# Small loads of four stages issued one stage earlier in a fused float32 network of attention, routing and spectral layers

## The reference, cut to what matters

```
x = x + neighbourhood_attention(gn(x)) ; x = x + conv_attention(gn(x))
t = tokens(x)
t = t + linear_attention(ln(t))     # q * sum over tokens of (k * v), with biases
t = t + spectral_ffn(ln(t))         # causal convolution with 16 filters by a transform over blocks,
                                    # mixing by 16 + 16 matrices, inverse transform, and a 3-tap part
t = t + causal_attention(ln(t))     # softmax(q k' / sqrt(128)) v over 4096 tokens
t = t + mixture_of_experts(ln(t))   # 8 experts, the best 2 of each token
```

## Time and profile before

| | |
|---|---|
| median of three runs | 3133.16 us |
| time of the profiled execution | 3134.44 us |
| its span, first to last instruction | 3132.4 us |
| TensorE busy | 2877.5 us (92%) |
| VectorE, ScalarE, GpSimd busy | 1936.2, 1436.2, 1073.7 us (62%, 46%, 34%) |
| mean granted clock of TensorE | 0.961 |
| data moved | 213.44 MB, 68 GB/s in the mean |

### The profile page before, as it was taken

One profiled execution on the slowest core, in us unless ns is written; L12 is line 12 of the kernel. 1 busy time (PEld: TensorE's weight loads), 2 busy tenths in 40 slices (PEclk: granted clock), 3 DMA queues, 4 the chain that ended last, 5 costly groups with the idle time before them and its releaser, 6 DMA issues. The chain is left out here.

```text
span 3132.4 us, 61484 instructions
## 1 busy us (share of the span) xinstructions
PE 2877.5 (92%) x23047; PEld 2223.5 (71%) x23047; DVE 1936.2 (62%) x3839; ACT 1436.2 (46%) x3076; POOL 1073.7 (34%) x1108
## 2 busy tenths in 40 slices
PE   5989999589987889999999999999779998999799
PEld 4667777334442558888988988888558887888455
DVE  5555558558846446666666666666457776776465
ACT  2545555321135325555555555555436665667200
POOL 3444445049923035555555555554100000000100
PEclk9999999789989799999999999999879999999899
DMA  7988784000003333444343443433200000000000
GB/s 165 176 175 169 171 172 129 1 14 1 1 3 118 141 66 80 86 85 88 79 88 81 89 88 80 89 81 65 65 7 1 1 1 1 1 1 1 10 22 31
DMA packets 419407, 213.44 MB, mean 68 GB/s; under 512 B 326260, under 2 KB 398604, under 8 KB 417324
## 3 DMA queue, kind: packets, MB, share of 16 engines
q1 hardware_dynamic: 401248, 199.32, 29.1%
q10 hardware_dynamic: 17868, 10.19, 1.7%
HBM read 177.82 MB, written 52.89 MB: 74 GB/s over the span
## 5 line engine op out<-in xcount | busy, mean ns | idle before, releaser
L1795 DVE TENSOR_TENSOR sl_vl_slot<-sl_psV_slot,sl_vh_slot 128x512 fp32r<-128x512 f32 x1024 | 636.1, 684 | 381.1 <-ACT sl_vh_slot L1777 380.8
L1777 ACT ACTIVATE sl_vh_slot<-sl_psV_slot 128x512 fp32r<-128x512 f32 x1024 | 529.5, 605 | 512.4 <-PE sl_psV_slot L1732 511.0
L1750 PE MATMUL sl_psY_slot<-sl_vl_slot,sp_Mh_sp 64*128 64x512 f32 x2048 | 417.2, 389 | 0.8 <-DVE sl_vl_slot L1795 0.3
L1750 PE MATMUL sl_psY_slot<-sl_vh_slot,sp_Ml_sp 64*128 64x512 f32 x2048 | 414.5, 386 | 0.0
L1750 PE MATMUL sl_psY_slot<-sl_vh_slot,sp_Mh_sp 64*128 64x512 f32 x2048 | 414.4, 386 | 0.0
L1708 POOL TENSOR_TENSOR sl_fl_slot<-sl_f_slot,sl_fh_slot 128x512 fp32r<-128x512 f32 x256 | 336.8, 1315 | 20.5
L1706 POOL CAST sl_fh_slot<-sl_f_slot 128x512 fp32r<-128x512 f32 x256 | 166.4, 650 | 451.2 <-PE sl_psV_slot L1732 450.0
L2191 DVE TENSOR_TENSOR ca_ptl_ca<-ca_psT_ca,ca_pth_ca 128x512 fp32r<-128x512 f32 (+1 forms) x272 | 183.8, 676 | 168.4 <-ACT ca_pth_ca L2128 168.3
L2128 ACT ACTIVATE ca_pth_ca<-ca_psT_ca 128x512 fp32r<-128x512 f32 (+1 forms) x272 | 158.8, 584 | 183.2 <-PE ca_psO_ca L87 179.2
L1750 PEld LDWEIGHTS sl_psY_slot<-sl_vl_slot,sp_Mh_sp 64*128 64x128 f32 x2048 | 207.8, 184 | 38.0 <-issue 12.7
L2255 POOL TENSOR_TENSOR ex_pick_ex<-ident 128x8 fp32r<-128x8 f32 x1 | 0.2, 203 | 665.0 <-POOLq L70 665.0
(11 more groups left out here) (397 smaller groups left out, 6260.6 us busy)
## 6 DMA issues: line engine op xcount, KB each, us to landing
sl_f_slot<-filt_hat SPq DMA_DIRECT2D x1024, 64.0 KB, 2.2
na_v_na<-na_windows SPq DMA_DIRECT2D x128, 390.0 KB
na_windows<-na_values SPq DMA_DIRECT2D x160, 113.8 KB, 7.9
na_values<-na_vo_na ACTq DMA_DIRECT2D x32, 260.0 KB, 9.0
u_hat<-fw_o_fwd SPq DMA_DIRECT2D x8, 1024.0 KB, 3.8
sl_u_slot<-u_hat SPq DMA_DIRECT2D x128, 64.0 KB, 2.2
y_hat<-sl_y_slot SPq DMA_DIRECT2D x128, 64.0 KB, 1.8
X<-in_x SPq DMA_DIRECT2D x8, 512.0 KB, 7.8
```

Of the source, the lines that this page charges most:

```text
L1750: mm = e.matmul(psY[half][:, :], left[pl][rows, :], right[pr][rows], start=kc == 0 and k == 0 and x == 0 and z == 0, stop=kc == KC - 1 and ...
L1777: e.activation(v_out(0, n, q), bank(4 * n + q), ACT.Copy).then_inc(S["v_high"], 1)
L1795: e.tensor_tensor(v_out(1, n, q), bank(m), v_out(0, n, q), ALU.subtract).then_inc(S["v_split"], 1)
```

## The change

Four groups of small loads move to the stage ahead of the one that uses them. `linear_attention` and `causal_attention` get their tiles from new helper classes; their normalisations run these helpers on SP. `c_fwd` is loaded at the end of `MixingWeights.sync`. `c_inv` is loaded in `spectral_slots` behind the first filter loads, and its product with `keep` becomes VectorE's last work there. Without being named in the title, EARLY goes from 8 to 4 in both spectral stages: `load_early` brings 4 slots (8 partitions, 256 KB) at a time, 15 times, and leaves 4 slots to the inverse transform.

```
+class LinearInputs:
+    engines = ("sync",)
+    names = ["la_loaded"]
+    def __init__(self, nc, T, ctx):
+        self.T, (sb, _) = T, allocator(nc, ctx, "_la")
+        self.w, self.bias = sb("la_w", [128, 3, 128]), sb("la_b", [128, 3])
+    def sync(self, e):
+        e.dma_start(self.w[:, :, :], self.T["la_w"]).then_inc(self.S["la_loaded"], 16)
+        e.dma_start(self.bias[:, :], self.T["la_b"]).then_inc(self.S["la_loaded"], 16)
+        e.wait_ge(self.S["la_loaded"], 32)
...
 def linear_attention
-            @block.sync
-            def _(e):
-                e.dma_start(w[:, :, :], T["la_w"]).then_inc(S["la_loaded"], 16)
-                e.dma_start(bias[:, :], T["la_b"]).then_inc(S["la_loaded"], 16)
-                e.wait_ge(S["la_loaded"], 32)      # on tensor, scalar and vector
...
 MixingWeights.sync, at its end
+        e.dma_start(self.G["fwd"][:, :, :], T["c_fwd"]).then_inc(S["fwd_loaded"], 16)
+        e.wait_ge(S["fwd_loaded"], 16)
...
 spectral_inputs
-                e.dma_start(fwd[:, :, :], T["c_fwd"]).then_inc(S["fwd_loaded"], 16)
-                e.wait_ge(S["fwd_loaded"], 16)     # on tensor
...
 spectral_slots
-    NPV, NFI, NFR, EARLY = 6, 2, 4, 8
+    NPV, NFI, NFR, EARLY = 6, 2, 4, 4
                 for n in range(NFR):
                     load_f(n)
+                e.dma_start(G["inv"][:, :], T["c_inv"]).then_inc(S["inv_loaded"], 16)
                 outputs(PAIRS - 1)                 # on vector
+                e.wait_ge(S["inv_loaded"], 16)
+                for z in range(2):
+                    e.tensor_tensor(G["kept"][:, z, :] ..., G["inv"] ..., G["keep"] ..., ALU.mult)
...
 spectral_outputs
-    EARLY, RB, NP, NT = 8, CH // NB, 4, 4
+    EARLY, RB, NP, NT = 4, CH // NB, 4, 4
-                e.dma_start(inv[:, :], T["c_inv"]).then_inc(S["inv_loaded"], 16)
-                e.wait_ge(S["inv_kept"], 2)        # on tensor
-                e.wait_ge(S["inv_loaded"], 16)     # on vector, and the two products
...
+class CausalInputs:                               # as LinearInputs, for ca_w and c_causal
...
 causal_attention
-                e.dma_start(w[:, :, :], T["ca_w"]).then_inc(S["ca_loaded"], 16)
-                e.dma_start(causal[:, :], T["c_causal"]).then_inc(S["ca_loaded"], 16)
-                e.wait_ge(S["ca_loaded"], 32)      # on tensor and vector
...
 build_program
-            layer_norm_channels(nc, T, X, into(Y), "la")
-            linear_attention(nc, T)
+            with ExitStack() as own:
+                inputs = LinearInputs(nc, T, own)
+                layer_norm_channels(nc, T, X, into(Y), "la", ahead=inputs)
+                linear_attention(nc, T, inputs)
...                                                 # and in the same way for causal attention
```

More of the change, by code:

```diff
@@ L735, in _ @@
                     helper.sync(e)
+            if helper and "gpsimd" in helper.engines:
                 @block.gpsimd
@@ L2483, in build_program @@
             T["Y"] = Y
-            layer_norm_channels(nc, T, X, into(Y), "ca")
-            causal_attention(nc, T)
+            with ExitStack() as own:
+                inputs = CausalInputs(nc, T, own)
+                layer_norm_channels(nc, T, X, into(Y), "ca", ahead=inputs)
+                causal_attention(nc, T, inputs)
             with ExitStack() as last:
```

52 lines of the change are left out of this document (32 added, 20 removed).

## The result

The changed kernel took 3122.16 us in the median of 7 runs (3119.89 to 3128.06); the kernel before, 3132.01 us (7 runs, 3128.76 to 3139.55). The ratio is 0.9968, with a 95% interval of 0.9956 to 0.998: 10 us faster, 0.32%, give or take 4. The forecast was 3124.6 us, in a range from 3119 to 3131. The profiled execution took 3124.49 us (span 3122.7).

What follows compares the result with a forecast made beforehand. TensorE, busy 92% of the span, was taken as the bound. Openings 9.4, less 0.4 for the inverse transform and 0.4 for the clock, gave 8.6 us off 3133.16: 3124.6 us, range 3119 to 3131.

Steps and rivals of the forecast that it cites:

- Three starts: Linear attention, forward transform and causal attention start 2.7, 2.1 and 4.6 us sooner with loads moved; sum 9.4 us.
- Rival (c): At the three openings, engines need the loads' time for something else; under 3 us gained, time 3131; chance 0.06.
- What pays for it: Stages that take over the moved loads: SP's extra issues and waits, some 0.9 us of issue, cost 0.
- Early loads: In the slots, going from 7 to 15 early loads, 0.4 us of issue each, costs 0.
- Rival (d): In the slots, early loads starve the filters; at 1.5 us each the time is 3147; chance 0.04.
- Inverse transform: Its start: 0.4 us gained without the products, 0.8 lost to later landing; -0.4 us, ends +2.8 and -1.2.
- a later landing: Inverse transform: the last 8 rows land 0.8 us later, the middle of "as now" and 1.6 later.
- far end: Inverse transform: latest landing of the last rows, 8.6 us, from batch 1's quickest load; 1.6 us later than now.
- Rival (a): Inverse transform: half the bytes land 2.4 us sooner, start 2.8 sooner; sum 11.8, time 3121.4; chance 0.13.
- Clock: TensorE's half clock behind restarts: linear attention loses 0.4 us, forward transform 0, causal attention 0 with 2 either way.
- I let it go to about 4.8: Linear attention: recovery to full clock grows from 4.0 to about 4.8 us, 0.8 more at half speed, cost 0.4.
- Rival (b): At the three starts, full clock returns no sooner than now; 4.7 us lost, sum 4.3, time 3128.9; chance 0.20.

Runs made afterwards that it cites:

- e3: Kernel before with only the loads of linear and causal attention moved, EARLY 8; 3125.38 us, ratio 0.9982 to the kernel before.
- e4: Kernel before with only `c_fwd`, `c_inv` and the products with `keep` moved, EARLY 8; 3132.47 us, ratio 1.0002 to the kernel before.
- e2: Kernel before with EARLY at 4 in both spectral stages, nothing else changed; 3134.78 us, ratio 1.0013 to the kernel before.
- e1: Changed kernel with EARLY back at 8; 3123.51 us, ratio 0.9972 to the kernel before.
- e7: Changed kernel with the last 8 rows spread over partitions 114 to 127 and loaded by two DMAs of 4 rows; 3122.7 us, ratio 0.997 to the kernel before.
- e5: Changed kernel with SP waiting for the last 8 rows before it issues batch 1's loads; 3124.07 us in a single run.
- e9: Changed kernel with extra unread products on TensorE in the tails of the four normalisations; 3121.83 us, ratio 0.9971 to the kernel before.
- e11: Changed kernel with extra unread TensorE products in the normalisations' tails, counts corrected, and in slots and inverse transform; 3111.78 us, ratio 0.9928 to the kernel before.
- e10: e7 with the second of its two 4-row loads issued by ScalarE in place of SP; 3116.17 us in a single run.

## Why the prediction was right, and where it was not

- **Three starts, 9.4 us.** 2.7, 2.0 and 4.6 us, 9.3 in all; e3 and e4 show that each hangs on its own load. Rival (c), an opening needed for something else, is out: TensorE starts within 0.8 to 1.3 us of VectorE's last instruction, as in the earlier trace rows.
- **What pays for it, nothing.** Normalisation and stage together are shorter by the opening or a little more, so the two loads beside a normalisation cost it nothing. `keep` behind the slots cost nothing either, and took 0.35 us there in place of 2.18; why it took so long beside the turns was not tested.
- **Early loads, nothing.** Rival (d) is out: no filter was late, the slots of e2 with 15 early loads are within 0.1 us of those of e1 with 7, and e7 with 30 issues has the shortest. The 0.4 us that came back in the slots (1057.6 to 1058.0) stand in e1, e3 and e4 too, which have EARLY at 8, and are absent in e5, with EARLY at 4; so they do not belong to the early loads.
- **Inverse transform, -0.4 us.** It came from +0.4 for the products and -0.8 for a later landing; both were mis-sized. The +0.4 took ScalarE's first turn for a third of a row of three, 1.94 us. In the kernel before that turn alone took 2.31 and ended at 2213.72, only 0.05 us ahead of the products:

```profile
2211.41 2.31 ACT L1850 ACTIVATE iv_t_inv<-sp_y_sp 128x1024 f32<-128x1024 f32 x1 [11.56 <-DMA sp_y_sp<-y_hat]
```

  With the products gone TensorE starts 0.1 us sooner behind that turn's start (2.33 us against 2.45). The later landing was there: 0.3 us in the changed kernel, 0.4 to 0.6 in e2, e9 and e11. (Its far end, 8.6 us, was counted from batch 1's own issue, which comes 0.85 us behind that of the rows.) Rival (a), by bytes, is out: 8, 16 and 32 rows land after 7.2, 6.9 and 7.45 us. That batch 1 presses on the rows is shown by e5, at 1.1 us; that it does so on the same partitions, and not on the queue or the memory it shares with them, is not separated. TensorE's start came 0.2 us later, against 0.4 forecast, since the two errors offset each other in part; the passage to the next normalisation is 0.6 us shorter, for the clock returned sooner.
- **Clock, -0.4 us.** The step that failed is "I let it go to about 4.8". With the load moved, linear attention was back at full clock after 3.0 to 4.25 us in eight profiles (read in steps of 0.25), without it after 3.5 to 4.25 in three: no growth. The forward transform came back after 2.75 to 4.25 us with, 4.25 to 5.0 without. A shorter pause left a shorter or equal half-clock stretch behind it, so in this profile the clock gave about 1 us in place of taking 0.4. Half of that belongs to the profile and not to the change: linear attention alone took 45.9 us here and 46.4 before, but 46.4 and 46.5 in e1 and e10, whose loads are moved too; the forward transform is some 0.5 us shorter in the mean of the profiles with the load moved. Rival (b), which priced the opposite at 4.7 us, is out. The price that the forecast gave the clock, half a microsecond for each microsecond at half clock, does hold: from the inverse transform's first product to the next normalisation the twelve profiles without extra products in between took 32.2 to 33.0 us, in the order of the clock's return, 2.8 to 4.7 us in.

The sum in place of 8.6: 9.3 from the openings, 1.9 from the clock and the inverse transform, 0.4 given back in the slots, 10.8 by the stage cuts. The medians say 9.9. That the forecast came this near has a share of luck: its two wrong terms, -0.4 each, are smaller than the noise, and the two ends that no edit touches took together 1109.5 to 1126.3 us in the eleven profiles of the first table.

## What to carry to other kernels

Behind a barrier, a load that the first instruction waits for costs the gap from the stage's opening to that instruction, here 2.0 to 4.6 us for loads of 128 to 256 KB; read it at the first instruction's bracket and move the load. Halving the last load and doubling the early ones was free and worthless here: 8, 16 and 32 rows landed within 6.8 to 7.5 us. Laying the 8 rows on partitions further apart halved the time of a packet, and holding back the load behind them brought 1.1 us; neither was seen in the time. When a change of 3 us does not show in a median, cut the profiles stage by stage, and look at the mean granted clock before believing a gain or a loss in code that was not touched.

## What the runs showed that I had not expected

- The mean granted clock of a run (0.958 to 0.964 without extra products) goes with the spread of single runs: over the 35 of before, spans of 3122.3 to 3138.7 us, it explains two thirds of the variance, in three other sets of 10 to 23 runs a quarter to two fifths. But raising it to 0.976 (e9) left the time as it was: it tells little of what the clock costs.
- An earlier return to full clock can be paid back: in experts it relapsed for 10 us in the seven profiles of the first table where it was back within 17.25 us, and in none of the four where it came later; 3 us between the two. e9, back after 16.0 us and without a relapse, shows that the time of the return alone does not decide it.
- Two loads of 4 rows, issued together on two queues, did not move together: 1.7 us between their first packets, and 1.9 on one queue. Each packet of the second began as one of the first ended; a second queue did not give the second load lanes of its own.
